# A graph layer's start: loads in the order of need, group 0's statistics on VectorE, counts by shifted matmuls, tests of the order later

## The reference

```python
h = jnp.maximum(_layernorm(x), 0.0)
W_rel = jnp.einsum('rb,bdf->rdf', w_comp, weight)          # 32 types from 8 bases
seg = etype * n_nodes + dst
agg = jax.ops.segment_sum(h[src] * norm, seg, num_segments=n_rels * n_nodes)
node_repr = jnp.einsum('rnd,rdf->nf', agg.reshape(n_rels, n_nodes, d_in), W_rel)
out = x + relu(node_repr + h_bias + h @ loop_weight)
```

## Time and profile before

| | before |
|---|---|
| median of three runs | 1020.2 us |
| lowest, highest | 1019.95, 1021.94 us |
| the profiled execution's own time | 1021.9 us |
| its span | 1020.1 us |
| TensorE matmuls busy | 991.9 us (97%) |
| VectorE busy | 956.9 us (94%) |
| ScalarE busy | 886.3 us (87%) |
| GpSimd busy | 724.5 us (71%) |

### The profile page before, as it was taken

One profiled execution on the slowest core, in us unless ns is written; L12 is line 12 of the kernel. 1 busy time (PEld: TensorE's weight loads), 2 busy tenths in 40 slices (PEclk: granted clock), 3 DMA queues, 4 the chain that ended last, 5 costly groups with the idle time before them and its releaser, 6 DMA issues.

```text
span 1020.1 us, 23782 instructions
## 1 busy us (share of the span) xinstructions
PE 991.9 (97%) x4903; PEld 576.0 (56%) x4903; DVE 956.9 (94%) x4368; ACT 886.3 (87%) x3251; POOL 724.5 (71%) x1282
## 2 busy tenths in 40 slices
PE   4899999999999999999999999999999999999996
PEld 2346565555555555656555555556565555555554
DVE  5999999999999999999999999999999999999994
ACT  6798989898989889898989898888989898989873
POOL 6887777777777677777777676777777777777730
PEclk9999999999999999999999999999999999999999
DMA  4455656556556556565565555555655655555544
GB/s 120 110 149 150 169 150 165 151 143 177 141 156 161 150 148 165 153 166 151 144 172 143 154 168 149 150 162 153 163 151 147 171 142 159 161 154 149 145 125 116
DMA packets 177887, 154.47 MB, mean 151 GB/s; under 512 B 17573, under 2 KB 150877, under 8 KB 177741
## 3 DMA queue, kind: packets, MB, share of 16 engines
q1 hardware_dynamic: 155885, 100.88, 35.3%
q0 software_dynamic: 20384, 51.32, 19.6%
q10 hardware_dynamic: 1472, 0.74, 0.3%
HBM read 101.31 MB, written 51.56 MB: 150 GB/s over the span
## 4 chain that ended last, share of the span: by engine, by line
PE 92%; DVE 3%; issue 2%; POOL 1%; DMA 1%; ACT 0%; DVEq 0%; POOLq 0%
PE y_ps L739 33%; PE y_ps L743 31%; PE win_ps L757 10%; PE win_ps L754 8%; PE hT_ps L801 4%; PE hT_ps L749 4%; PE mix_ps L793 1%; DVE sum_a L952 1%; POOL xg L543 1%; DVE sum_b L952 1%; DMA xg<-x,idx 1%; DVE msg L985 0%; DMA src_all<-src 0%; DVE nstats L1035 0%; DVE res L1070 0%
## 5 line engine op out<-in xcount | busy, mean ns | idle before, releaser
L543 POOL DMA_INDIRECT xg<-x,idx x392 | 383.1, 977 | 73.5 <-issue 33.9
L739 PE MATMUL y_ps<-w_all,hT 128*128 128x512 f32 x784 | 412.2, 607 | 5.0 <-DVE sum_a L952 4.9
L743 PE MATMUL y_ps<-w_all,hT 128*128 128x512 f32 x784 | 400.3, 592 | 0.0
L490 POOL TENSOR_TENSOR u<-z 128x128 f32<-128x128 f32 x392 | 180.1, 459 | 183.8 <-ACT z L591 179.8
L591 ACT ACTIVATE z<-y_ps,mix 128x128 f32<-128x128 f32 x784 | 244.4, 366 | 45.0 <-PE y_ps L743 44.7
L952 DVE SCALAR_TENSOR_TENSOR sum_b<-y_ps,mix,sum_b 128x128 f32<-128x128 f32 x784 | 264.3, 337 | 0.0
L743 PEld LDWEIGHTS y_ps<-w_all,hT 128*128 128x128 f32 x784 | 149.1, 190 | 187.9 <-issue 161.1
L739 PEld LDWEIGHTS y_ps<-w_all,hT 128*128 128x128 f32 x784 | 132.3, 189 | 120.6 <-DVE sum_a L952 66.7
L587 ACT ACTIVATE z<-y_ps,mix 128x128 f32<-128x128 f32 x392 | 140.7, 359 | 66.2 <-PE y_ps L739 64.9
L625 ACT ACTIVATE hw<-xw,shift,nrstd 128x128 f32<-128x128 f32 x391 | 192.3, 493 | 0.4 <-DVE shift L1052 0.4
L952 DVE SCALAR_TENSOR_TENSOR sum_b<-y_ps,mix,z 128x128 f32<-128x128 f32 x392 | 130.8, 334 | 38.5 <-ACT z L587 38.3
(11 more groups left out here) (99 smaller groups left out, 1158.8 us busy)
## 6 DMA issues: line engine op xcount, KB each, us to landing
seg<-msgs SPq DMA_DIRECT2D x391, 104.8 KB
msgs<-msg SPq DMA_DIRECT2D x98, 258.0 KB
xw<-x POOLq DMA_DIRECT2D x97, 256.0 KB, 3.1
out<-res SPq DMA_DIRECT2D x97, 256.0 KB, 2.8
type_bc<-type_rows SPq DMA_DIRECT2D x56, 112.0 KB
xg<-x,idx POOLq DMA_INDIRECT x392, 3.2
w_all<-weight ACTq DMA_DIRECT2D x1, 512.0 KB, 7.7
dst_i<-dst ACTq DMA_DIRECT2D x1, 196.0 KB, 2.5
```

Source lines behind the costliest of these rows:

```text
L490: nc.gpsimd.tensor_tensor(u[:, r, :], z[:, r, 0, :], z[:, r, 1, :], ALU.add).then_inc(s_u, 1)
L543: nc.gpsimd.indirect_dma_start(xg[:, q, j, :], None, x, bass.IndirectOffsetOnAxis(ap=idx[:, q, j:j + 1], axis=0)).then_inc(s_gather[q * G ...
L739: nc.tensor.matmul(y_ps[2 * t % 5][:, :, :], hT[:, q, j, :], w_all[:, B // 2:B, :], start=True, stop=True).then_inc(s_y_high, 1)
L743: nc.tensor.matmul(y_ps[(2 * t + 1) % 5][:, :, :], hT[:, q, j, :], w_all[:, 0:B // 2, :], start=True, stop=True).then_inc(s_y, 1)
```

## The change

First loads: SP sends the first 8 columns of src and of norm, the types of groups 0 and 1 in four pieces, and the rest of src. Then it waits for gather 1 of group 0 (counted from 0) and sends w_all, which leaves ScalarE's queue; it waits for gather 3 and sends the rest of norm, dst_c and the types of groups 2 to 6. dst_far is loaded with the node constants behind the messages of group 1. TensorE waits for w_all only ahead of the first products.

Group 0's statistics are all VectorE's, in the order in which the gathers land; ScalarE's relus of group 0 stand between its sign passes, and its step 0 is written out. `gains(1)` moves on GpSimd from behind the third gather of step 3 to behind the first.

Counts: one one-hot of a partition's first bin (`first_hot`, shifted by up to SPAN columns when read) is the moving operand, and the counts (`in_bin16`) are the weights, one matmul for each shift. The eight `bin_count` passes and the matmul on `bad16` go. `row_table` makes scan, minimum and table between step 0 and step 1 on VectorE. `half_off`, `cap` and `cz` are made before dst has landed.

Tests: `check_order` and the tests of `row_step` become nine `order_step`s, in steps 20, 23 and so on to 44. CROWD_STEP becomes 48, the mode is chosen in step 49 and stored in step 52.

```diff
 OUT_AT = 5
-MODE_STORE = 40
+MODE_STORE = 52
 SPAN = 8
-CROWD_STEP = 18
-ROW_STEPS = 9
+CROWD_STEP = 48
+ORDER_FROM = 20
+ORDER_EVERY = 3
+ORDER_STEPS = 9
 
 
 def sweep(eng, count, step, ring=RING, peel=5, first=0):
...
+                load_type_rows(c % 2, 2 if c == 0 else 0, groups, c * TYPES, s_types[c % 2])
+
+            def load_type_rows(half, lo, hi, g, done):
                 for j in range(G):
-                    sp.dma_start(type_bc[R * j:R * j + R, c % 2, 0:groups, :],
-                                 type_rows[j:j + 1, c * TYPES:c * TYPES + groups, :].to_broadcast([R, groups, P])
-                                 ).then_inc(s_types[c % 2], 16)
+                    sp.dma_start(type_bc[R * j:R * j + R, half, lo:hi, :],
+                                 type_rows[j:j + 1, g + lo:g + hi, :].to_broadcast([R, hi - lo, P])).then_inc(done, 16)
 
             sp.dma_start(src_all[:, 0:FIRST], src[:, 0:FIRST]).then_inc(s_src_first, 16)
+            sp.dma_start(norm_all[:, 0:FIRST], norm[:, 0:FIRST]).then_inc(s_norm_first, 16)
+            load_type_rows(0, 0, 2, 0, s_types_first)
             sp.dma_start(src_all[:, FIRST:NT], src[:, FIRST:NT]).then_inc(s_src, 16)
+            sp.wait_ge(s_gather[1], 16)
+            sp.dma_start(w_all[:, :, :], weight.rearrange("b d f -> d b f")).then_inc(s_all, 16)
+            sp.wait_ge(s_gather[G - 1], 16)
+            sp.dma_start(norm_all[:, FIRST:NT], norm[:, FIRST:NT]).then_inc(s_norm, 16)
+            sp.dma_start(dst_c[:, :], dst_cols).then_inc(s_dst_c, 16)
             load_types(0)
-            sp.dma_start(norm_all[:, :], norm).then_inc(s_norm, 16)
-            sp.dma_start(dst_c[:, :], dst_cols).then_inc(s_dst_c, 16)
-            sp.dma_start(dst_far_i[:, :], dst_far).then_inc(s_far, 16)
 
             def store_messages(g, n, q):
                 sp.wait_ge(s_msg, g * G + G)
@@ -386,6 +400,7 @@
                     load_node_constants()
 
             def load_node_constants():
+                sp.dma_start(dst_far_i[:, :], dst_far).then_inc(s_far, 16)
...
             def gains(g, q):
-                if is_before(g, 1):
+                if g == 0:
+                    pool.wait_ge(s_norm_first, 16)
+                if g == 2:
                     pool.wait_ge(s_norm, 16)
...
-                    if j == 2 and 3 <= g < NG + 2:
+                    if j == (0 if g == 3 else 2) and 3 <= g < NG + 2:
                         gains(g - 2, (q - 2) % RING)
...
-            act.dma_start(w_all[:, :, :], weight.rearrange("b d f -> d b f")).then_inc(s_weights, 16)
...
-            for k in range(SPAN):
+            def sign(k):
                 nc.scalar.activation(signs[:, k, :], dst_f[:, :], ACT.Sign, bias=limits[:, k:k + 1], scale=-1.0,
                                      accum_out=below_sum[:, k:k + 1]).then_inc(s_below, 1)
-            group_means(0, 0, 0)
-            group_squares(0, 0)
-            sweep(act, STEPS, step)
+
+            def first_relu(j):
+                nc.scalar.activation(h[:, 0, j, :], xg[:, 0, j, :], ACT.Relu, bias=neg_mean[:, 0, j:j + 1]).then_inc(s_relu, 1)
+
+            for k in range(SPAN - 2):
+                sign(k)
+            act.wait_ge(s_mean_first, 1)
+            first_relu(0)
+            first_relu(1)
+            sign(SPAN - 2)
+            sign(SPAN - 1)
+            act.wait_ge(s_mean, 1)
+            first_relu(2)
+            first_relu(3)
+            nc.scalar.activation(std[:, 0, :], nmv[:, NRING - 1, :, 1], ACT.Sqrt, bias=eps_col[:, 0:1]).then_inc(s_std, 1)
+            act.wait_ge(s_hT, 1)
+            nc.scalar.activation(hT[:, 0, :, :], hT_ps[:, :, :], ACT.Copy).then_inc(s_hT_sb, 1)
+            group_means(1, 0, 1)
+            group_squares(1, 1)
+            sweep(act, STEPS, step, first=1)
...
             def count_bins(half):
                 counts = win_ps[0:1, :, :].rearrange("p b f -> p (b f)")
+                pe.wait_ge(s_first_hot, 1)
                 pe.wait_ge(s_bins, half + 1)
                 for k in range(half * (SPAN // 2), (half + 1) * (SPAN // 2)):
-                    nc.tensor.matmul(counts[:, 0:BINS], ones16[:, :], bin_count[:, k, :],
-                                     start=k == 0, stop=k == SPAN - 1)
+                    mm = nc.tensor.matmul(counts[:, 0:BINS], in_bin16[:, k:k + 1], first_hot[:, SPAN - k:SPAN - k + BINS],
+                                          start=k == 0, stop=k == SPAN - 1)
                 if half == 1:
-                    nc.tensor.matmul(counts[:, BINS:BINS + 1], ones16[:, :], bad16[:, :],
-                                     start=True, stop=True).then_inc(s_hist, 1)
-
-            pe.wait_ge(s_weights, 16 * 2)
+                    mm.then_inc(s_hist, 1)
+
+            pe.wait_ge(s_weights, 16)
...
+                        if g == 1 and j == 0:
+                            pe.wait_ge(s_all, 16)
...
+            nc.vector.memset(first_hot[:, 0:SPAN], 0.0)
+            nc.vector.memset(cz[:, 0:F], 0.0)
+            nc.vector.memset(cz[:, F:C], -1.0).then_inc(s_front, 1)
...
+            nc.vector.tensor_copy(half_off[:, :, 0], win_off[:, 0:NGW * G])
+            nc.vector.tensor_scalar(half_off[:, :, 1], win_off[:, 0:NGW * G], float(HALF), None, ALU.add)
+            nc.vector.tensor_scalar(cap[:, :], win_off[0:1, :], float(G * P * AHEAD - SEG_P - (G - 1) * P), None, ALU.add)
...
-
-            def check_order():
-                nc.vector.tensor_tensor(falls[:, 0:NT - 1], dst_f[:, 0:NT - 1], dst_f[:, 1:NT], ALU.is_gt)
-                nc.vector.tensor_tensor(falls[:, NT - 1:NT], dst_f[:, NT - 1:NT], next_f[:, :],
-                                        ALU.is_gt).then_inc(s_step, 1)
-                dve.wait_ge(s_step, 7)
-                nc.vector.tensor_reduce(bad[:, 0:1], falls[:, :], AX_X, ALU.max).then_inc(s_step, 1)
+                nc.vector.tensor_scalar(first_hot[:, SPAN:SPAN + BINS], bin_n[:, :], first_binf[:, 0:1], None,
+                                        ALU.is_equal).then_inc(s_first_hot, 1)
 
             def bin_counts(half):
...
+                    nc.vector.tensor_scalar(in_bin16[:, 0:1], below_sum[:, 0:1], 0.5, NT / 2, ALU.mult, ALU.add)
                 nc.vector.tensor_tensor(in_bin[:, lo1:hi], below_sum[:, lo1:hi], below_sum[:, lo1 - 1:hi - 1],
                                         ALU.subtract).then_inc(s_share, 1)
-                dve.wait_ge(s_share, 2 * half + 1)
-                nc.vector.tensor_scalar(in_bin[:, lo1:hi], in_bin[:, lo1:hi], 0.5, None, ALU.mult).then_inc(s_share, 1)
-                if half == 1:
-                    dve.wait_ge(s_step, 9)
-                    nc.vector.tensor_tensor(bad16[:, :], bad[:, 0:1], bad[:, 1:2], ALU.max)
-                dve.wait_ge(s_share, 2 * half + 2)
-                for k in range(lo, hi):
-                    ins = nc.vector.tensor_scalar(bin_count[:, k, :], bin_n[:, :], bins[:, k:k + 1], in_bin[:, k:k + 1],
-                                                  ALU.is_equal, ALU.mult)
-                ins.then_inc(s_bins, 1)
-
-            def copy_hist():
+                dve.wait_ge(s_share, half + 1)
+                nc.vector.tensor_scalar(in_bin16[:, lo1:hi], in_bin[:, lo1:hi], 0.5, None, ALU.mult).then_inc(s_bins, 1)
+
+            def row_table():
                 dve.wait_ge(s_hist, 1)
-                nc.vector.tensor_copy(hist[:, :], win_ps[0:1, :, :].rearrange("p b f -> p (b f)")[
...
+                nc.vector.tensor_copy(hist[:, :], win_ps[0:1, :, :].rearrange("p b f -> p (b f)")[:, 0:BINS]).then_inc(s_meta, 1)
+                dve.wait_ge(s_meta, 1)
+                nc.vector.tensor_tensor_scan(upto[:, :], ones_row[:, :], hist[:, :], 0.0, ALU.mult, ALU.add).then_inc(s_step, 1)
+                dve.wait_ge(s_step, 7)
+                nc.vector.tensor_tensor(start_c[:, :], upto[:, :], cap[:, :], ALU.min).then_inc(s_step, 1)
+                dve.wait_ge(s_step, 8)
+                nc.vector.tensor_scalar(row_tab[:, :], start_c[:, :], float(EP - SEG_P), float(FRONT - SEG_P),
+                                        ALU.min, ALU.add).then_inc(s_start, 1)
+
+            def order_step(k):
 
                 if k == 0:
-                    dve.wait_ge(s_meta, 1)
...
+                elif k == 2:
+                    dve.wait_ge(s_step, 10)
+                    nc.vector.tensor_tensor(falls[:, :], dst_i[:, :], dst_far_i[:, :], ALU.is_equal).then_inc(s_step, 1)
+                elif k == 3:
+                    dve.wait_ge(s_step, 11)
+                    nc.vector.tensor_reduce(bad[:, 0:1], falls[:, :], AX_X, ALU.max).then_inc(s_step, 1)
+                elif k == 4:
+                    dve.wait_ge(s_step, 12)
+                    nc.vector.tensor_tensor(falls[:, 0:NT - 1], dst_f[:, 0:NT - 1], dst_f[:, 1:NT], ALU.is_gt)
+                    nc.vector.tensor_tensor(falls[:, NT - 1:NT], dst_f[:, NT - 1:NT], next_f[:, :],
+                                            ALU.is_gt).then_inc(s_step, 1)
                 elif k == 5:
+                    dve.wait_ge(s_step, 13)
```

(47 more changed lines are left out.)

51 lines of the change are left out of this document (15 added, 36 removed).

## The result

The changed kernel took 1018.8 us (median of nine runs, 1017.5 to 1019.7), the kernel before 1020.2 in nine runs beside it: a ratio of 0.9975, with a 95% interval of 0.9965 to 0.9985. By the ratio the kernel is 2.5 us faster (1.5 to 3.6), of the 4.2 forecast, which puts it at 1017.7, inside the range of 1014.3 to 1018.7. The ratio is not the quotient of the two medians: these are only 1.4 us apart, and 1018.8 itself lies 0.1 us above the range: the nine runs of before fall into five of 1019.6 to 1020.2 and four of 1021.9 to 1022.1, so their median is an unsteady number. The profiled execution took 1018.97 us, its span is 1017.2; against the profiled one of before (1021.9 and 1020.1) that is 2.9 less.

What follows compares the result with a forecast made beforehand. TensorE was taken as the bound, gapless from 66.96 us, so only the start could gain. Terms -2.9 -1.5 +0.2 gave -4.2 us, forecasting 1016.0 from the 1020.2 median; range 1014.3 to 1018.7.

Steps and rivals of the forecast that it cites:

- Bound and place: TensorE is gapless from the second node transposes at 66.96 us; gain must come before, where some 6.9 us are gaps.
- the late loads: norm, dst_c and types, issued from 10.9 to 13.7 us while gathers 6 to 8 are under way: 0.2 us lost.
- The first products: Start of TensorE's products: gather 4 lands at 10.8, w_all about 12.5, first product at 14.6, 3.0 us earlier.
- How much arrives: From first product to sum_a of tile 4: u 4 at 30.6, sum_a at 31.1, 2.9 us earlier.
- GpSimd is the later: At u 0: GpSimd's queue, not z of tile 0 (done at 18.6), sets it, at 19.05 instead of 21.15.
- the rival that gave gather 8 6.2 us: Late loads hit gather 8: lands at 19.6, gain only 1.4 us, 1018.8; halfway 1017.5; chance 0.12.
- VectorE's steps: Behind tile 4 VectorE sets the pace; minimum and half_off (1.0), table and dst_far shift (0.25 each) leave: 1.5 us.
- The stretched gather: A gather at 39.85 took 1.86 us instead of 0.97; half_off was blamed, and moving it early costs nothing.
- The rival took the whole 0.9 us: Scan or minimum holds a gather near 17 us: gain only 3.3 us, 1016.9; chance 0.15.
- gain 1: On GpSimd from 28.43 to about 23; with VectorE's passes leaving step 1 about 3 us, all but 0.8 lost.
- Row table: Scan, minimum and table on VectorE between histogram and step 1, 15.6 to 17.9 us, hidden by 0.2.
- Tests at cost 0: Tests spread over groups 20 to 44, 4.6 us of VectorE passes, covered by its idle time: cost 0.

Runs made afterwards that it cites:

- gain_old: Changed kernel with gain 1 back behind the third gather of step 3: 1018.89 us, ratio 0.9978 to the kernel before.
- both load edits: Changed kernel with w_all issued without a wait and the rest of the loads behind gather 8: 1017.42 us, 0.9960; on another chip 1018.25, 0.9971.
- w_all_first: Changed kernel with w_all sent at the start from ScalarE's queue, as before the change: 1018.02 us, ratio 0.9971.
- rows_in_steps: Changed kernel with scan, minimum and table back at the ends of VectorE's steps 1 to 3, half_off beside the minimum: 1020.68 us, ratio 0.9992.
- more_tests: Changed kernel with two more 0.56 us VectorE passes beside each of the nine test steps: 1024.18 us, ratio 1.0040.
- the repeat: The changed kernel measured again without any edit: 1019.26 us, ratio 0.9976 to the kernel before.

## Why the prediction was right or wrong

**Bound and place: right.** The gain lies before the gapless part and is the shift of the second node transposes, 3.2 us where 4.4 was forecast there (4.2 with the late loads). The sum was -2.9 +0.2 -1.5; the marks show -2.45 for the first two terms and -0.76 for the third.

**The first products: the step that failed in its mechanism.** "Gather 4 at 10.8", reckoned with the 2.8 us of a lone gather. It took 4.4, because w_all was issued in the same moment; the step had cleared w_all as a load that could come late itself and never asked what it does to the gather beside it. w_all was early (12.4, as forecast), the gather was late, and the product came at 16.51 instead of 14.6. With w_all out of the way the same working gives the measured 14.2 to 14.7 in four kernels.

**How much arrives: right in kind, 0.45 too high.** u 4 to sum_a and u 0 to u 4 (11.49; forecast 11.55) are as written, and gain_old shows that u 4 sets sum_a. But for u 0 "GpSimd is the later" failed: its queue was free at 18.95, the 19.05 of the forecast, and z of tile 0 was the later. u 0 was 19.55 for 19.05, since gather 8 was held too (4.1 us; ScalarE waited until 17.49, product and gather together put z of tile 0 at 18.57 for 17.7). The late loads were priced at 0.2 on the sum, and the rival that gave gather 8 6.2 us left -1.4 in all; gather 8's 4.1 us lie between that and the 2.8. In the two kernels with both load edits, and in w_all_first, sum_a of tile 4 was at 31.07 to 31.11, the forecast's 31.1.

**VectorE's steps: 1.5 forecast, 0.76 arrived** (32.98 us from sum_a of tile 4 to the second node transposes before, 32.21 to 32.24 after, in all kernels that keep the row passes out). This is the larger error of the sum. The rows tell where it went, from one sum_a to the next. Minimum and half_off pay in full: their place, between sum_a of tiles 6 and 7, shrinks from 3.18 us to 2.15. Before:

```profile
37.84 0.33 DVE L952 SCALAR_TENSOR_TENSOR sum_a<-y_ps,mix,u 128x128 f32<-128x128 f32 x1
...
41.02 0.33 DVE L952 SCALAR_TENSOR_TENSOR sum_a<-y_ps,mix,u 128x128 f32<-128x128 f32 x1
```

The shift of dst_far pays its 0.25 too (2.51 to 2.23). The table, counted at 0.25, pays nothing (2.50 and 2.56): in its stead VectorE waits 0.20 at 44.60 in the changed kernel. And 0.39 is taken back by two messages that grow beside GpSimd's u, 0.23 between tiles 4 and 5 and 0.16 between tiles 7 and 8: the one at 32.76 took 0.50 where 0.28 is usual, with u of tile 5 on GpSimd from 32.63 to 33.10, the one at 38.99 took 0.45, with u of tile 8 from 38.82 to 39.28. Before the change no message of this stretch grew. The rest, 0.1, is spread in small differences. So the step failed in taking the table as time of the path, and in taking it that nothing new would come up once VectorE is earlier. rows_in_steps agrees: minimum and half_off cost 1.03 again and the table nothing, and the second message, now elsewhere, gives 0.16 back, 0.87 in all. That the u stretches the message is read from their meeting in three places, not tested.

**The stretched gather: wrong reason, no cost.** The prediction laid it on half_off; the scan alone does it too (1.60), and where it falls between u 0 and u 4 it costs, as rows_in_steps shows (0.67). The rival took the whole 0.9 us for a gather near 17. It was held by 0.2 (1.17 at 17.78), as only 0.4 us of the scan was left when it started, and u 0 waited for z anyway. The Trainium skill (SBUF — State Buffer, "SBUF: two separate sides") names VectorE's passes in a two-port mode, and those with two SBUF inputs if GpSimd reads SBUF, as ones that keep GpSimd out to their end; the scan has two SBUF inputs, and the stretch of 0.63 us of the 0.82 that were left of it agrees with that, but for the last 0.2.

**gain 1: 0.8 us forecast with the scan's leaving, and had, but from the scan.** u 4 to sum_a of tile 4 went from 1.28 to 0.50 us. gain_old (gain late, scan gone) and rows_in_steps (gain early, scan back) both have 0.50. But from u 0 to sum_a of tile 4, 12.83 us before and 11.98 after, the first has 12.00 and the second 12.66: with the gain early the scan no longer holds VectorE up, it holds a gather and with it u 4. Only the scan's leaving brings the time, and beside it the gain's move is worth nothing.

**Row table: later than forecast** (done at 19.2 for 17.9, as the counts were late) and hidden by the slack ahead of sum_a. **Tests at cost 0: right,** with less to spare than was said: VectorE's 0.4 us in each period, shown by more_tests.

**From the sum to the time.** Sum by the marks: -2.45 -0.76 = -3.2, within the interval of the ratio, 1.5 to 3.6 us, about its 2.5. The first pairs of products (1.12 to 2.08 us) and the end (11.3 to 14.5 us for the same code) differ from execution to execution, by up to 1 and 3 us, so a median of three runs was no firm base: with 21 to 33 runs beside the later kernels, the kernel before had medians of 1020.8 to 1021.3. Faster is clear, as the whole interval of the ratio lies below 1; by over 0.2%, as forecast, is only its middle (0.25%, from 0.15 to 0.35). The place inside the range owes something to the base: counted in absolute time from the low median of three runs, the same kernel is just outside.

## What to carry to other kernels

A transfer that is moved to "when the first ones have landed" starts beside the next ones: look which wanted transfer is issued in that moment, and put the late load behind the last one that the path needs, or at the very start, where it delays only one that has slack. Removed passes count in full only where their engine sets the pace just there (minimum and half_off did, the table didn't), and an engine that is earlier meets others at new places; take one back and measure what it costs. Idle time of an engine that is spread in small pieces covers only work in pieces of that size: here 0.56 us a step went in free, 1.1 us more cost 0.62.

## What was not expected of the hardware

The first pair of 128x512 matmuls took 1.1 to 2.1 us at a granted clock given as 1.00, differently in executions of the same kernel, and idle matmuls before them did not mend it: twenty were followed by a granted clock of 0.50, and the kernel lost 5.6 us. At the end the sums ran at half pace in some executions, in the changed kernel's profile with the clock at 0.70 (mean from 1005 to 1010) and 0.50 behind that:

```profile
1006.87 1.86 PE L790 MATMUL win_ps<-seg,pick 105*64 105x128 f32 x16
1009.61 1.62 PE L787 MATMUL win_ps<-w_loop,hwT 128*128 128x128 f32 x6 [0.88 <-DVE res L1097]
```

The same sums took 1.10 and 0.91 in the profile of the repeat, at 1.00. And one gather beside a 512 KB load took 4.1 to 4.8 us, against 2.5 to 2.9 with less or nothing beside it.
